# Earlier weight checks on VectorE in group 0, and three steps of GpSimd at other places of the expert stage, in a two-layer gated transformer kernel

## The chip, the cores and the metric

The kernel runs on one core of a Trainium2 chip. The metric is the device time of one execution in microseconds (us), as the median of three. TensorE is called PE below, VectorE DVE, ScalarE ACT, GpSimd POOL, and the queue of SyncE, which issues most of the DMAs, SP.

## The reference

There are T = 2048 tokens of D = 256. Layer 0 is an attention over 64 context keys and a mixture of 16 experts with two chosen for each token; layer 1 is a linear map with a context row and a dense FFN with a hidden width of 1024, whose weights are ternary (-1, 0, 1).

```python
x = x + tanh(g_xattn[0]) * L0_xattn(layernorm(x), ctx, ctx, Wq, bq, Wk, bk, Wv, bv)
x = x + tanh(g_ffn[0])   * L0_ffn(layernorm(x), gate_w, w1, w3, w2)      # 16 experts, top 2
x = x + tanh(g_xattn[1]) * L1_xattn(layernorm(x), ctx, W, b)
x = x + tanh(g_ffn[1])   * L1_ffn(layernorm(x), w1_w, w1_s, ..., w3_w, w3_s)

def L1_ffn(x, ...):                       # tlin(x, w, s) = (x @ w.T) * s
    h = silu(tlin(x, w1_w, w1_s)) * tlin(x, w2_w, w2_s)      # 256 -> 1024
    h = gelu(tlin(h, h1_w, h1_s))                            # 1024 -> 1024
    h = gelu(tlin(h, h2_w, h2_s))                            # 1024 -> 1024
    return tlin(h, w3_w, w3_s)                               # 1024 -> 256
```

## The kernel before

Everything runs in one program, written out by hand for each engine; the order on an engine is the order in which its code is written, and engines wait for each other on semaphores. Three stages follow each other.

**Attention and routing** (to about 76 us) work on four groups of 512 tokens.

**The expert stage** (about 76 to 173 us) is a loop over 47 blocks of 128 rows (`NBLK`) on every engine. POOL gathers the rows of block i (line 641, indirect DMA, into six buffers) once PE has transposed block i-6; PE transposes them, applies the expert's three matrices, and ACT writes the result out, which SP stores. Other work is hung into this loop at fixed block numbers: the tables of lines 62 to 66 say at which i an engine does it. On POOL these are `root_half` (line 566, a power that makes 1/sqrt of a variance; `ROOT2_AT` for the third layer norm, `ROOT3_AT` for the fourth) and `add_row_half` (line 627, adds the context row `crow` to two tiles of X; `ROW_AT`). Each has two halves, q = 0 and 1, and each waits for its own input: `root_half(3, 0)` for the variance that DVE makes in `statistics3_half(0)` at i = 35, `root_half(2, 1)` for the one of i = 37, `add_row_half(1)` for PE's transposes of i = 37. Their results are wanted by `x3_half(1)` (DVE, i = 41) and `normalise4_half(0)` (DVE, i = 43).

**The FFN stage** (from 173 us to the end) works on four groups g of 512 tokens, each with a gated first layer (layer 0 here), `layer` 1, `layer` 2 and the last map to 256 columns. The activations are kept as a high and a low part in fp32r, so each weight tile is used by two matmuls. In layers 1 and 2 PE fills a PSUM bank m by 16 matmuls (lines 1987 and 1988), ACT applies the gelu (line 1533) into one of three buffers `sg`, and DVE makes the high part (`CAST`, line 1259) and the low part (`TENSOR_TENSOR`, line 1261), after which it counts `f_hl[m]` up. The first bank of the next layer needs all eight of these, one by one (line 1986). ACT may run three banks ahead of DVE.

Hung into DVE's loop in group g are steps for the next group: `x2(g + 1)` after m = 1 of layer 1 (lines 1188 to 1194: adds the gathered expert rows to X, one `n_x2` for each of four tiles, and statistics), `low3` after m = 7, `x3` and `normalise4` in layer 2. PE's transposes `T3(g + 1)` stand after m = 6 of layer 1 and wait for those four `n_x2` (line 1902). POOL then makes `root(2, g + 1)` and `add_row(g + 1)` (lines 690 and 691, 128x1024 elements).

The weights come as 44 panels of 128x512 fp32 (256 KB each). SP loads them raw in order (`load_raw`, line 356: at most four on the way); panels 22 to 43 only once PE has finished layer 0 of group 0 (line 482). ACT and DVE round them to fp32r in place. Since rounding loses nothing only where the weights are simple numbers, the kernel checks that: SP loads each panel a second time into one of two buffers `stage` (`load_check`, line 485, all behind the last raw panel in SP's queue; load w waits until check w-2 is done), and DVE compares it with the rounded panel (`check_panel`, line 1229) and writes the count of differences. There are 11 checks a group (`NCHK`), 44 in all; the last ones raise a flag that would start a slower general path. In group 0 the 11 checks stand behind banks m = 5, 6, 7 of layer 1 and all eight of layer 2; in groups 1 to 3 behind all eight of layer 1 and m = 0, 1, 2 of layer 2.

Of the kernel before, what the change touches and what calls it, by code (L numbers as in the profile page):

```python
# [43 lines left out]
FK = F // P  # L44
# [15 lines left out]
JW = DK * P + H  # L60

Y_AT = (28, 29, 31, 32, 34, 35, 37, 38)
ROOT2_AT, ROW_AT, ROOT3_AT = (37, 45), (38, 45), (44, 46)
ADD_AT, STAT_AT = (25, 28, 31, 36), (26, 29, 33, 37)
TURN3_AT, HIGH3_AT, LOW3_AT, PART_AT, X3_AT = (30, 37), (31, 38), (32, 39), (33, 40), (34, 41)
NORM_AT, TURN4_AT, HIGH4_AT, LOW4_AT = (43, 45), (44, 47), (45, 48), (46, 48)
# [4 lines left out]
NCHK = 11  # L71
# [38 lines left out]
def flamingo_kernel(nc, x, ctxT, cols, rows, wq, wkT, wvT, gate, experts, w1T, w2T, panels, consts, identity, out):  # L110
    with ExitStack() as ctx:
# [629 lines left out]
        def _(eng):  # L741
# [446 lines left out]
            def x2(g):  # L1188
                for j in range(TG):
                    row_added(g, j)  # L1190
                    row_statistics(g, j)
                own.done()
                eng.wait_ge(ln_rstd[2], counted(g - 1))
                eng.tensor_scalar(veps[:, 2, :], mv[:, 2, :, 1], EPS, None, ALU.add).then_inc(ln_var[2], 1)

            def low3(g):
                for k in range(DK):
                    eng.wait_ge(n_h3, DK * g + k + 1)
                    ins = eng.tensor_tensor(xTl[:, k, :], bank[6 + k][:, :], xTh[:, k, :].bitcast(F32), ALU.subtract)
                    if k < DK - 1:  # L1200
                        own(ins)
                ins.then_inc(n_l3, 1)

            def x3(g):
                def make(j):
                    if j == 0:
                        eng.wait_ge(n_row, counted(g))
                        eng.wait_ge(ln_rstd[2], counted(g))
                    if j % 2 == 0:
                        eng.wait_ge(n_p1, 2 * g + j // 2 + 1)  # L1210
                    own(eng.scalar_tensor_tensor(tiles(g)(j), bank[6 + j // 2][:, (j % 2) * D:(j % 2 + 1) * D],
                                                 rstd[:, 2, j:j + 1], tiles(g)(j), ALU.mult, ALU.add))

                statistics(eng, own, tiles(g), 3, g, make)

            def normalise4(g):
                eng.wait_ge(ln_rstd[3], counted(g))
                eng.wait_ge(n_T4, counted(g - 1))
                for j in range(TG):
                    eng.tensor_scalar(xn[:, j, :], tiles(g)(j), mv[:, 3, j, 0:1], rstd[:, 3, j:j + 1],  # L1220
                                      ALU.subtract, ALU.mult).then_inc(n_xn, 1)
# [7 lines left out]
            def check_panel(w):  # L1229
                if w >= DVE_PAN:  # L1230
                    eng.wait_ge(act_pan, w + 1 - DVE_PAN)
                eng.wait_ge(dma_chk[w % 2], 16 * (w // 2 + 1))
                to, _ = panel(w)
                eng.scalar_tensor_tensor(stage[:, w % 2, :], stage[:, w % 2, :], 1.0, to.bitcast(F32), ALU.mult,
                                         ALU.not_equal, accum_out=diff[:, w:w + 1]).then_inc(dve_chk, 1)

            def ffn(g, more, general):
# [14 lines left out]
                for layer, h in ((1, hB), (2, hA)):  # L1252
                    for m in range(FK):
                        if layer == 1 and m == 0:

                            eng.wait_ge(f_dma, 16 * g + 16 if g < NG else OUT_DONE + 32 * (g - NG))
                        r = (8 * layer + m) % 3
                        eng.wait_ge(f_act[m], g3 + (layer + 2))
                        own(eng.tensor_copy(h[0][:, m, :], sg[:, r, :]))  # L1259
                        own.done()  # L1260
                        eng.tensor_tensor(h[1][:, m, :], sg[:, r, :], h[0][:, m, :].bitcast(F32),
                                          ALU.subtract).then_inc(f_hl[m], 1)
                        if more and layer == 1 and m == 1:
                            x2(g + 1)
                        if more and layer == 1 and m == 7:
                            low3(g + 1)
                        if more and layer == 2 and m == 2:
                            x3(g + 1)
                        if more and layer == 2 and m == 3:
                            normalise4(g + 1)  # L1270

                        c = 8 * (layer - 1) + m - (FK + FK - NCHK if g == 0 else 0)
                        if not general and 0 <= c < NCHK:
                            check_panel(NCHK * g + c)
                            if NCHK * g + c == NPAN - 1:
                                eng.wait_ge(dve_chk, NPAN)
                                own(eng.reduce_max(flagf[:, 0:1], diff[:, :], AX.X))
                                own.done()
                                eng.tensor_scalar(flagf[:, 0:1], flagf[:, 0:1], 1.0, None, ALU.min).then_inc(dve_flag, 1)
# [28 lines left out]
            for g in range(NG):  # L1308
                ffn(g, g < NG - 1, False)
            eng.wait_ge(pool_flag, 1)  # L1310
            general = eng.value_load(flag[0:1, 0:1], min_val=0, max_val=1)
# [804 lines left out]
```

## Time and profile before

| | |
|---|---|
| median of 3 runs | 519.88 us (518.80 to 521.58) |
| profiled execution | 519.88 us, span 517.8 us |
| PE busy | 485.9 us (94% of the span) |
| DVE busy | 312.4 us (60%) |
| ACT busy | 214.4 us (41%) |
| POOL busy | 149.5 us (29%) |
| TensorE clock granted, mean | 0.974 of full speed |

The span is the time from the first to the last instruction of the profiled execution; 2.1 us of its device time lie around it. Busy time of PE is modelled for pipelined matmuls, so neighbouring matmuls overlap in it. The chain that ended last says which engine a microsecond of delay would have to be on to count; the timelines say what each engine did when, and what it waited for before that. All times in timelines and windows count from the start of the span.

### The profile page before, as it was taken

Reading aid. Unit: us, or ns where it says so; the run is one execution under the profiler, and the core shown is the slowest. Engines: PE = TensorE matmul, PEld = TensorE weight load, DVE = VectorE, ACT = ScalarE, POOL = GpSimd, SP = SyncE. Lnnn points to the kernel's source line nnn. Section 1 sums busy time; section 2 is a strip of 40 time slices with the busy share of each in tenths; the row PEclk is TensorE's granted clock in tenths of the full one; section 3 lists DMA queues with packets and bytes.
Section 4 is the critical chain, followed back from the end, with each engine's and each line's share of the span. In section 5 each row is a group of like instructions: output and inputs, shape, how many; then the busy total and the mean of one; then the engine's idle time right before and its main releaser. Section 6 shows DMA issues by size and latency. Waiting matters only on the chain.

```text
span 517.8 us, 7829 instructions
## 1 busy us (share of the span) xinstructions
PE 485.9 (94%) x2750; PEld 417.0 (81%) x2750; DVE 312.4 (60%) x836; ACT 214.4 (41%) x444; POOL 149.5 (29%) x159
## 2 busy tenths in 40 slices
PE   8898978996899889999999999999999999999996
PEld 8697768885789668888987888897888888788886
DVE  3568876673588566557455964626677634645433
ACT  4379914663467676532245121226322123611210
POOL 1867856656762320201062110116011101000000
PEclk9799977998899999999999999999999999999999
DMA  8945833786672548521141121005032002022101
GB/s 296 330 169 161 282 100 100 198 289 181 198 213 84 184 135 281 163 82 41 42 128 57 52 71 42 0 2 162 22 99 64 0 1 81 3 72 70 42 1 47
DMA packets 34465, 58.82 MB, mean 114 GB/s; under 512 B 4529, under 2 KB 18353, under 8 KB 34354
## 3 DMA queue, kind: packets, MB, share of 16 engines
q1 hardware_dynamic: 29760, 47.12, 27.8%
q0 software_dynamic: 3840, 10.49, 7.4%
q10 hardware_dynamic: 818, 0.61, 0.4%
q8 instruction: 25, 0.41, 0.3%
q14 instruction: 22, 0.18, 0.1%
HBM read 47.85 MB, written 14.42 MB: 120 GB/s over the span
## 4 chain that ended last, share of the span: by engine, by line
PE 84%; DVE 7%; issue 2%; ACT 2%; another core or an unknown queue 1%; DMA 1%; POOL 1%; SPq 0%; DVEq 0%; POOLq 0%
PE bank L1987 23%; PE bank L1988 22%; PE bank L1959 5%; PE bank L1956 5%; PE bank L1559 4%; PE bank L1561 4%; PE bank L1560 4%; PE bank L2020 3%; PE bank L2019 3%; PE bank L1805 2%; PE bank L1645 2%; PE bank L1808 1%; DMA gw<-gate 1%; PE bank L1619 1%
## 5 line engine op out<-in xcount | busy, mean ns | idle before, releaser
L1533 ACT ACTIVATE sg<-bank,colv 128x512 f32<-128x512 f32 x64 | 44.1, 690 | 177.2 <-PE bank L1988 177.2
L1987 PE MATMUL bank<-Ah,Wr 128*128 128x512 f32 x256 | 100.3, 392 | 0.4 <-DVE sg L1242 0.4
L1987 PE MATMUL bank<-Bh,Wr 128*128 128x512 f32 x256 | 99.9, 390 | 0.0
L1988 PE MATMUL bank<-Al,Wr 128*128 128x512 f32 x256 | 99.7, 390 | 0.0
L1988 PE MATMUL bank<-Bl,Wr 128*128 128x512 f32 x256 | 99.7, 389 | 0.0
L1559 PE MATMUL bank<-EL,turned 128*128 (+1 forms) x141 | 47.4, 336 | 12.1 <-ACT yb L1465 9.3
L1987 PEld LDWEIGHTS bank<-Ah,Wr 128*128 128x128 f32 x256 | 48.1, 188 | 11.7 <-DVE sg L1242 1.3
L1988 PEld LDWEIGHTS bank<-Bl,Wr 128*128 128x128 f32 x256 | 48.1, 188 | 9.8
L1988 PEld LDWEIGHTS bank<-Al,Wr 128*128 128x128 f32 x256 | 48.1, 188 | 9.8
L1987 PEld LDWEIGHTS bank<-Bh,Wr 128*128 128x128 f32 x256 | 48.1, 188 | 9.8
L1259 DVE CAST Ah<-sg 128x512 fp32r<-128x512 f32 x32 | 13.6, 426 | 60.0 <-ACT sg L1533 60.0
L564 POOL TENSOR_TENSOR rstd<-veps,mhalf 128x4 f32<-128x4 f32 x6 | 8.4, 1401 | 116.7 <-DVE veps L738 61.1
L1560 PE MATMUL bank<-EH,turned 128*128 (+1 forms) x141 | 41.7, 295 | 0.0
L1077 DVE TENSOR_TENSOR turned<-bank,turned 128x384 fp32r<-128x384 f32 (+2 forms) x51 | 26.6, 523 | 25.0 <-ACT turned L1451 13.9
L1561 PE MATMUL bank<-EH,turned 128*128 (+1 forms) x141 | 41.6, 295 | 0.0
L1559 PEld LDWEIGHTS bank<-EL,turned 128*128 128x128 f32 x141 | 28.6, 203 | 15.2 <-issue 14.7
L1242 DVE SCALAR_TENSOR_TENSOR sg<-bank,colv,sg 128x512 f32<-128x512 f32 x32 | 24.0, 751 | 25.7 <-ACT sg L1519 20.5
L1519 ACT ACTIVATE sg<-bank,colv 128x512 f32<-128x512 f32 x32 | 22.1, 689 | 41.0 <-PE bank L1959 36.9
L1956 PE MATMUL bank<-xTh,Wr 128*128 128x512 f32 x96 | 37.7, 393 | 0.0
L1959 PE MATMUL bank<-xTl,Wr 128*128 128x512 f32 x96 | 37.6, 392 | 0.0
L1259 DVE CAST Bh<-sg 128x512 fp32r<-128x512 f32 x32 | 13.6, 426 | 39.8 <-ACT sg L1533 39.8
L641 POOL DMA_INDIRECT xg<-xb_dram,perm x32 | 30.9, 965 | 17.0 <-PE bank L1808 7.6
(280 smaller groups left out, 1031.2 us busy)
## 6 DMA issues: line engine op xcount, KB each, us to landing
Wraw<-panels SPq DMA_DIRECT2D x44, 256.0 KB
stage<-panels SPq DMA_DIRECT2D x44, 256.0 KB
ES<-experts SPq DMA_DIRECT2D x16, 384.0 KB, 4.9
ys_dram<-yb SPq DMA_DIRECT2D x47, 128.0 KB
ys_dram<-x SPq DMA_DIRECT2D x1, 1920.0 KB, 8.4
X<-x SPq DMA_DIRECT2D x3, 512.0 KB, 7.8
xb_dram<-xb SPq DMA_DIRECT2D x3, 512.0 KB, 5.3
out<-outb SPq DMA_DIRECT2D x3, 512.0 KB
```

The source lines that it names most:

```text
L641: eng.indirect_dma_start(out=rows, out_offset=None, in_=xb_dram, in_offset=bass.IndirectOffsetOnAxis(ap=perm[:, i:i + 1], axis=0)).then_in ...
L1077: eng.tensor_tensor(t_low[b][:, w], bank_t[b][:, w], t_high[b][:, w].bitcast(F32), ALU.subtract).then_inc(b_xl, 1)
L1242: eng.scalar_tensor_tensor(sg[:, m % 3, :], bank[2 * (m % 2) + 1][:, :], colv[:, C_S2 + m:C_S2 + m + 1], sg[:, m % 3, :], ALU.mult, ALU.mu ...
L1259: own(eng.tensor_copy(h[0][:, m, :], sg[:, r, :]))
L1533: eng.activation(sg[:, (8 * layer + m) % 3, :], bank[m % 4][:, :], ACT.Gelu, scale=colv[:, c + m:c + m + 1]).then_inc(f_act[m], 1)
L1559: mm(dst, lhs[0], rhs[1], start=first, stop=False)
L1560: mm(dst, lhs[1], rhs[0], start=False, stop=False)
L1561: return mm(dst, lhs[0], rhs[0], start=False, stop=last)
L1956: mm(dst, w[:, u, k, :], x_high[:, k, :], start=k == 0, stop=False)
L1959: ins = mm(dst, w[:, u, k, :], x_low[:, k, :], start=False, stop=k == DK - 1 and not general)
L1987: mm(bank[m % 4][:, :], Wr[:, base:base + P], h[0][:, k, :], start=k == 0, stop=False)
L1988: ins = mm(bank[m % 4][:, :], Wr[:, base:base + P], h[1][:, k, :], start=False, stop=k == FK - 1 and not general)
```

## The change

Two things are changed. In the expert stage three of POOL's steps stand at other blocks: `root_half(2, 1)` and `add_row_half(1)` come at i = 44 in place of 45, and `root_half(3, 0)` at i = 42 in place of 44. In the FFN stage the 11 checks of group 0 stand where those of the other groups stand: behind m = 0 to 7 of layer 1 and m = 0, 1, 2 of layer 2. The number of checks, their order, the loads on SP and all other engines' code are as before.

```diff
-ROOT2_AT, ROW_AT, ROOT3_AT = (37, 45), (38, 45), (44, 46)
+ROOT2_AT, ROW_AT, ROOT3_AT = (37, 44), (38, 44), (42, 46)
...
-                        c = 8 * (layer - 1) + m - (FK + FK - NCHK if g == 0 else 0)
-                        if not general and 0 <= c < NCHK:
+                        c = 8 * (layer - 1) + m
+                        if not general and c < NCHK:
                             check_panel(NCHK * g + c)
```

What now stands in a row on DVE, in group 0, layer 1, between bank 0 and bank 1 (Bh and Bl are the high and low part of the output of layer 1; `stage` is the buffer of the second load):

```order
 L1259 CAST Bh_53<-sg_58 128x512
 L1261 TENSOR_TENSOR Bl_54<-sg_58,Bh_53 128x512
+L1234 SCALAR_TENSOR_TENSOR stage_61,diff_88<-stage_61,Wr_49 128x512
 L1259 CAST Bh_53<-sg_58 128x512
 L1261 TENSOR_TENSOR Bl_54<-sg_58,Bh_53 128x512
```

The first check comes in between them; behind bank 1 follows `x2(1)`.

DVE before, in the same layer, from the end of `x2(1)` (its last tile's sums and statistics, then the variance `veps`) to bank 2:

```order
L1093 SCALAR_TENSOR_TENSOR X_55<-xn_59,wtop_83,X_55 128x256
L1096 SCALAR_TENSOR_TENSOR X_55<-y2_60,wtop_83,X_55 128x256
L1101 BN_STATS stats_70<-X_55 128x6
L1103 BN_AGGR mv_71<-stats_70 128x2
L1194 TENSOR_SCALAR veps_72<-mv_71 128x4
L1259 CAST Bh_53<-sg_58 128x512
L1261 TENSOR_TENSOR Bl_54<-sg_58,Bh_53 128x512
```

And now:

```order
L1093 SCALAR_TENSOR_TENSOR X_55<-xn_59,wtop_83,X_55 128x256
L1096 SCALAR_TENSOR_TENSOR X_55<-y2_60,wtop_83,X_55 128x256
L1101 BN_STATS stats_70<-X_55 128x6
L1103 BN_AGGR mv_71<-stats_70 128x2
L1194 TENSOR_SCALAR veps_72<-mv_71 128x4
L1234 SCALAR_TENSOR_TENSOR stage_61,diff_88<-stage_61,Wr_49 128x512
L1259 CAST Bh_53<-sg_58 128x512
L1261 TENSOR_TENSOR Bl_54<-sg_58,Bh_53 128x512
L1234 SCALAR_TENSOR_TENSOR stage_61,diff_88<-stage_61,Wr_49 128x512
```

The check of bank 1 stands behind `x2(1)`, and each of banks 2, 3 and 4 has one behind its pair, where there was none. Five checks have left the banks of layer 2 from m = 3 on.

POOL in the expert stage, from the gather of block 39 to the end of the loop (xg and xg_more are the buffers of the gathers, two adjacent gathers stand in one row with x2):

```order
 L641 DMA xg_173<-xb_dram,perm_85 128x256 x2
 L641 DMA xg_more_174<-xb_dram,perm_85 128x256 x2
+L569 TENSOR_TENSOR rstd_73<-veps_72,mhalf_74 128x2
 L641 DMA xg_173<-xb_dram,perm_85 128x256 x2
 L569 TENSOR_TENSOR rstd_73<-veps_72,mhalf_74 128x2
-L641 DMA xg_173<-xb_dram,perm_85 128x256
-L569 TENSOR_TENSOR rstd_73<-veps_72,mhalf_74 128x2
 L630 TENSOR_TENSOR X_55<-X_55,crow_69 128x512
-L641 DMA xg_173<-xb_dram,perm_85 128x256
+L641 DMA xg_173<-xb_dram,perm_85 128x256 x2
 L569 TENSOR_TENSOR rstd_73<-veps_72,mhalf_74 128x2
```

`root_half(3, 0)` now stands ahead of the gathers of blocks 43 and 44, and `root_half(2, 1)` and the context row's addition ahead of those of blocks 45 and 46.

## Rows read from the trace of the kernel before

**Rows 1.** The page: the chain that ended last by engine (section 4), one group (section 5).

```profile
PE 84%; DVE 7%; issue 2%; ACT 2%; another core or an unknown queue 1%; DMA 1%; POOL 1%; SPq 0%; DVEq 0%; POOLq 0%
...
L564 POOL TENSOR_TENSOR rstd<-veps,mhalf 128x4 f32<-128x4 f32 x6 | 8.4, 1401 | 116.7 <-DVE veps L738 61.1
```

**Rows 2.** Timeline of SP: start us, us, engine, line, operation, out<-in, count.

```profile
174.79 34.38 SPq L360 DMA_DIRECT2D Wraw<-panels  x28
...
209.22 0.91 SPq L488 DMA_DIRECT2D stage<-panels  x2
```

**Rows 3.** Busy time by window: DMA share and GB/s are the last two columns.

```profile
209.00:213.00 4.00, 4.00 (x19) 3.32 (x18) 1.12 (x2) 2.62 (x5) 0.00 (x0) 1.00 0.90 292
213.00:213.50 0.50, 0.50 (x4) 0.40 (x3) 0.24 (x1) 0.50 (x2) 0.00 (x0) 1.00 0.49 188
```

**Rows 4.** Timeline of DVE, layer 1 of group 0; in brackets idle time before, and releaser.

```profile
199.22 0.69 DVE L1261 TENSOR_TENSOR Bl<-sg,Bh 128x512 fp32r<-128x512 f32 x1
199.83 0.48 DVE L1093 SCALAR_TENSOR_TENSOR X<-xn,wtop,X 128x256 f32<-128x256 f32 x1
...
205.05 0.48 DVE L1096 SCALAR_TENSOR_TENSOR X<-y,wtop,X 128x256 f32<-128x256 f32 x1
...
206.33 0.42 DVE L1259 CAST Bh<-sg 128x512 fp32r<-128x512 f32 x1
...
214.33 0.69 DVE L1234 SCALAR_TENSOR_TENSOR stage<-stage,Wr 128x512 f32<-128x512 f32 x1
```

**Rows 5.** Timeline of DVE, layer 2 of group 0.

```profile
228.70 0.43 DVE L1259 CAST Ah<-sg 128x512 fp32r<-128x512 f32 x1 [1.86 <-ACT sg L1533]
...
242.76 0.68 DVE L1234 SCALAR_TENSOR_TENSOR stage<-stage,Wr 128x512 f32<-128x512 f32 x1
...
244.43 0.69 DVE L1234 SCALAR_TENSOR_TENSOR stage<-stage,Wr 128x512 f32<-128x512 f32 x1
```

**Rows 6.** Timeline of PE, end of layer 1 and first bank of layer 2, group 0.

```profile
215.97 1.04 PE L1904 MATMUL bank<-ident,X 128*128 128x128 f32 x8
...
223.69 0.39 PE L1987 MATMUL bank<-Bh,Wr 128*128 128x512 f32 x1
```

**Rows 7.** Timelines of DVE and POOL where POOL adds a context row.

```profile
155.10 1.55 DVE L1056 TENSOR_SCALAR X<-X,alpha,beta 128x256 f32<-128x256 f32 x1
...
158.50 0.40 DVE L1056 TENSOR_SCALAR X<-X,alpha,beta 128x256 f32<-128x256 f32 x1
...
217.09 2.49 POOL L676 TENSOR_TENSOR X<-X,crow 128x1024 f32<-128x1024 f32 x1 [9.24 <-PE bank L1904]
217.36 2.77 DVE L1261 TENSOR_TENSOR Bl<-sg,Bh 128x512 fp32r<-128x512 f32 x1
220.05 0.68 DVE L1234 SCALAR_TENSOR_TENSOR stage<-stage,Wr 128x512 f32<-128x512 f32 x1
```

**Rows 8.** Timeline of SP, and narrow windows (GB/s last), around two transfers that ran alone.

```profile
174.00:174.25 0.25, 0.25 (x3) 0.21 (x2) 0.00 (x0) 0.00 (x0) 0.00 (x0) 1.00 0.62 201
...
174.79 0.33 SPq L360 DMA_DIRECT2D Wraw<-panels  x1
...
215.06 0.33 SPq L488 DMA_DIRECT2D stage<-panels  x1
...
217.00:217.25 0.25, 0.25 (x3) 0.21 (x2) 0.25 (x1) 0.25 (x1) 0.16 (x1) 1.00 0.21 74
```

**Rows 9.** Busy time by window in the block stage: PEclk is third from the end.

```profile
119.60:124.00 4.40, 0.80 (x7) 0.59 (x6) 0.56 (x1) 0.61 (x2) 2.25 (x3) 1.00 0.53 161
125.80:129.00 3.20, 3.20 (x17) 3.20 (x17) 1.73 (x4) 1.46 (x4) 1.77 (x3) 0.50 0.84 232
74.50:84.40 9.90, 8.11 (x48) 7.53 (x46) 3.36 (x14) 2.47 (x7) 5.68 (x6) 0.50 0.27 79
```

**Rows 10.** Timelines of DVE and PE in the block stage.

```profile
151.27 0.17 DVE L1108 TENSOR_SCALAR veps<-mv 128x2 f32<-128x2 f32 x1
...
162.29 0.38 PE L1805 MATMUL bank<-ident,xg 128*128 128x128 f32 x2
```

## The prediction

> **What bounds the kernel now.** I read the page's chain first: it lies on PE for 84% of the span [rows 1], so an edit on another engine counts only where it makes PE wait. Then I asked, for each moved step, which transfer or engine it waits for and who waits behind it. In the FFN stage that led from DVE to SP's queue. SP issues the last 28 raw panels from 174.79 to 209.17 without a pause worth naming, and only then, at 209.22, the first two loads of the checks [rows 2]. The first check ran at 214.33, right behind DVE's own work for bank 5 of layer 1 [rows 4], and waited for nothing. The change asks for its data one bank ahead of the pair that was over at 199.83 [rows 4], so before 197. SP's code is the same, and its loads hang on PE and on the panels, so they do not come earlier. DVE will stand still for them, with the low parts of layer 1 behind it.
>
> **When the first check can run (T0).** At 209.22 raw panels and two check loads are on the way together: 292 GB/s from 209 to 213 and 188 GB/s in the next half microsecond, where it runs out [rows 3]. The last 256 KB are those of the second check load: 94 KB of them in that half microsecond, the other 162 KB at 292 GB/s take 0.55 us, so the first load's last byte comes at 212.45. From last byte to a released wait I take the store that ran alone: it moved its last bytes before 174.25 and SP went on at 174.79, 0.5 us later [rows 8]. T0 = 213.0. Bounds: 212.5 (no such delay) and 214.3 (the check did run then).
>
> **DVE from T0 on**, all of it work that waits ready, since ACT may be three banks ahead:
> - Check 0, 0.61 us, and the pair of bank 1, 1.07 us. A check and a pair together are 244.43 - 242.76 = 1.67 us [rows 5]; a pair without its check is what is left, and the check's own share is that of its start to the next start, as for the TENSOR_TENSOR 199.22 to 199.83 [rows 4]. `x2(1)` starts at 214.7.
> - `x2(1)`: 206.33 - 199.83 = 6.5 us [rows 4], to 221.2. Its fourth `n_x2` comes 205.05 + 0.48 - 199.83 = 5.7 us after its start, at 220.4. PE's T3 started at 215.97 before [rows 6] and waits for that: PE is about 4 us late at bank 7.
> - Six times check and pair (checks 1 to 6, banks 2 to 7), 10.0 us, to 231.2.
> - POOL's `root(2, 1)`, 1.4 us [rows 1], starts when `x2(1)` is over, and its context row, 2.49 us [rows 7], follows it (T3 is over by then). This now falls into DVE's hurry, from 222.7 to 225.2, where check 2 is due at 222.9. In the trace a TENSOR_TENSOR that should take 0.69 us took 2.77 beside that same addition, and the next started 0.47 us after the addition's end [rows 7]. So DVE goes on at 225.7 in place of 223.5: +2.2 us. Bounds: 0, and 2.2. I take the upper one since a TENSOR_SCALAR with one tensor was held as well (1.55 us for 0.40, beside the half-size addition of the expert stage [rows 7]), so all of DVE's operations here look exposed.
> - The low part of bank 7 is there at 231.2 + 2.2 = 233.4, and 0.2 us more for its end and the handover: 233.6.
>
> The Trainium skill (SBUF — State Buffer, section "SBUF: two separate sides") says that VectorE and GpSimd share one pair of SBUF ports as an exclusive lock, which a VectorE operation with two SBUF inputs or in a two-port mode needs and which whoever starts first keeps for the whole instruction. By that rule the check itself, with two SBUF inputs, is held and the addition costs the full 2.2 us; had only the pair's TENSOR_TENSOR been held, as the row alone shows, it would be the one of bank 3, due at 223.9, and the cost 1.1 us. The rows are with the rule.
>
> **Does the load of each check keep up?** SP issued load 2 at 215.06, 0.73 us after check 0 started [rows 4, 8]; its last bytes moved before 217.25 [rows 8], and with 0.5 us for the wait it is ready about 3.3 us after the check two places before. Two steps of DVE are 3.34 us. It just fits; if a load takes 0.3 us more, three pairs of steps cost +0.9. I take 0 and keep 0.9.
>
> **What PE sees.** Layer 2's first bank needs the low parts one by one. Its last two matmuls started at 223.69 [rows 6] and now start at 233.6: **+9.9 us**. The 4 us at T3 are part of that, not beside it. All later matmuls follow back to back, and nothing later on PE has slack to give back. In layer 2 DVE waited 1.86 us for a gelu although it had a check there [rows 5], so it gets level in one or two banks, and the five checks that leave layer 2 free time that nobody waits for: 0.
>
> **PE's clock.** PE stands or works thinly from 216 to 220 and again from 226 to 233. Before, after the thin stretch 119.6 to 124.0 (0.80 us busy in 4.4), the granted clock was 0.50, that is 1.2 GHz, from 125.8 to 129.0 [rows 9]. A first slow stretch of that length would lie in the time in which PE is paced by DVE, and costs nothing; a second one, begun by the pacing, reaches into dense matmuls, where each microsecond of it costs half. Bounds 0 and half of 3.2, 1.6; I take the middle, **+0.8**.
>
> **The steps on POOL in the expert stage.** `root_half(3, 0)` now waits for a variance that DVE writes at 151.27 [rows 10], ahead of the gather of block 43; the gathers of 45 and 46 come behind `root_half(2, 1)` and the addition. By the rows I estimate the gather of 45 some 4 us later than before, at about 157.2; a lone 256 KB load needed 2.2 us to its last byte [rows 8], 0.5 for the wait, and the gather moves half as much, so it is there by 161, ahead of PE's transposes at 162.29 [rows 10]. No wait is added. DVE's steps stand where they stood, and the earlier half of the root is wanted only at block 43. If the addition, which moves by about half a microsecond, no longer holds DVE at 155.10 [rows 7], up to 0.3 us is gained; a gather that does come late costs about as much as it is late, 1 us at the most. I take 0.
>
> **Sum.** The profiled execution took 519.88 us, which is also the median of the three. 519.88 + 9.9 + 0.8 = **530.6 us**.
>
> **Rivals.**
> - *Short.* The addition on POOL holds nobody, the first load is there at 212.5, the clock does not fall into dense work: 519.88 + 9.9 - 2.2 - 0.5 = 527.1. For it: only one kind of pair was seen held here. Against: both rows of [rows 7].
> - *Long.* PE's clock stays down. Before, it stayed at 0.50 for 9.9 us, from 74.5 to 84.4, with PE 8.1 us busy in it [rows 9]. If such a stretch begins in the pacing and lies over 5 to 8 us of dense work, it costs 2.5 to 4 us in place of 0.8, with the loads' 0.9 at most beside it: 532.3 to 534.7. Against: the more usual stretches are of 3.2 us.
> - *Not slower.* DVE's wait for the first check is covered. The place is `dma_chk[0]` behind bank 0 of layer 1. The last low part of layer 1 comes 20.6 us after T0, and PE wanted it at 223.69, so up to T0 = 203.1 the change costs nothing, and from there on each microsecond of T0 costs one. Then only the expert stage's steps are left: 519.6 to 519.9. Against: the load is not even issued by 209.22 [rows 2], and nothing in the change moves that. It would need the second load of a panel to come out of SP's queue ahead of the raw ones.
>
> **How the numbers follow.** Forecast (528 to 532.3): 0.75. Short (below 528, but slower): 0.09. Long: 0.12. Not slower: 0.04. The range of 527.3 to 533.5 takes in the lower bounds of T0 and of the addition together, and above it 1.3 us of T0, the rest of the clock's 1.6 and a part of the loads' 0.9. A measurement of this kernel can tell about 0.5% from no change, 2.6 us. All cases but the last are above that: slower 0.96, within 0.03, faster 0.01.
>
> **What the changed kernel's profile would show.** DVE idle for some 16 us ahead of the first L1234, which starts near 213.0 and has the DMA as its releaser; PE's T3 late by about 4 us, waiting on DVE's L1096; the PE matmuls of layer 2's first bank spread over some 8 us, with waits on DVE's L1261; POOL's L676 with a DVE operation of over 2 us beside it; PEclk at 0.50 somewhere between 221 and 238; from the second bank of layer 2 on every row of PE later by the same 10 to 11 us. In the expert stage every row of PE as before within 0.3 us. The prediction is wrong if the first L1234 starts before 210, if PE goes on into layer 2 while DVE still makes the low parts, or if PE's delay shrinks again in groups 1 to 3.

## The result, and the profile after

The changed kernel takes 535.49 us (median of 4 runs, 533.00 to 536.22) against 520.34 us of the kernel before on the same chip (4 runs, 518.80 to 521.58): ratio 1.028 (1.024 to 1.033), so 12 to 17 us slower. The sign and the mechanism of the prediction hold, its size doesn't: 530.6 us was forecast, with a range up to 533.5. The profiled execution took 533.13 us, its span is 531.0 us. Medians here and below are taken over all runs of a kernel, ratios without those runs that lie more than 1.5% above its fastest.

The page of the changed kernel: the chain that ended last, by engine, and the group of the checks.

```profile
PE 76%; DVE 9%; DMA 6%; issue 3%; ACT 3%; another core or an unknown queue 1%; POOL 1%; SPq 1%; DVEq 0%; POOLq 0%
...
L1234 DVE SCALAR_TENSOR_TENSOR stage<-stage,Wr 128x512 f32<-128x512 f32 x44 | 32.4, 735 | 17.9 <-DMA stage<-panels 17.8
```

PE's share of the chain fell from 84% [rows 1] to 76%, those of DVE and DMA grew, and all 44 checks together waited 17.9 us for loads, 17.8 of them in one place. The timelines of SP and DVE show that place (in layer 1 of group 0; the columns are those of [rows 4]).

```profile
174.05 35.16 SPq L360 DMA_DIRECT2D Wraw<-panels  x28
...
195.23 0.69 DVE L1261 TENSOR_TENSOR Bl<-sg,Bh 128x512 fp32r<-128x512 f32 x1
213.69 0.69 DVE L1234 SCALAR_TENSOR_TENSOR stage<-stage,Wr 128x512 f32<-128x512 f32 x1 [17.77 <-DMA stage<-panels]
...
215.38 0.48 DVE L1093 SCALAR_TENSOR_TENSOR X<-xn,wtop,X 128x256 f32<-128x256 f32 x1
...
221.87 0.69 DVE L1234 SCALAR_TENSOR_TENSOR stage<-stage,Wr 128x512 f32<-128x512 f32 x1
...
223.55 2.88 DVE L1234 SCALAR_TENSOR_TENSOR stage<-stage,Wr 128x512 f32<-128x512 f32 x1
...
226.36 0.41 DVE L1259 CAST Bh<-sg 128x512 fp32r<-128x512 f32 x1
...
233.51 0.69 DVE L1261 TENSOR_TENSOR Bl<-sg,Bh 128x512 fp32r<-128x512 f32 x1
```

SP is through with the raw panels at 209.21, where it was at 209.17 before [rows 2], and issues the first load of a check at 209.26. DVE had been ready at 195.9 and stands still for 17.77 us. Then it works off `x2(1)` and the pairs and checks one behind the other up to 234.2. The check at 223.55 takes 2.88 us where its neighbours take 0.69. The reason stands in POOL's timeline:

```profile
222.05 1.41 POOL L564 TENSOR_TENSOR rstd<-veps,mhalf 128x4 f32<-128x4 f32 x1 [37.31 <-DVE veps L1194]
223.45 2.42 POOL L676 TENSOR_TENSOR X<-X,crow 128x1024 f32<-128x1024 f32 x1
```

PE's timeline in the same stretch: the transposes T3 (L1903), then the end of layer 2's first bank.

```profile
216.52 0.41 PE L1903 MATMUL bank<-ident,X 128*128 128x128 f32 x2 [1.12 <-DVE X L1096]
...
221.14 0.69 PE L1903 MATMUL bank<-ident,X 128*128 128x128 f32 x2 [0.88 <-DVE X L1096]
...
230.90 0.50 PE L1986 MATMUL bank<-Bh,Wr 128*128 128x512 f32 x1 [0.94 <-DVE Bl L1261]
...
232.58 0.54 PE L1986 MATMUL bank<-Bh,Wr 128*128 128x512 f32 x1 [0.94 <-DVE Bl L1261]
...
234.26 0.80 PE L1986 MATMUL bank<-Bh,Wr 128*128 128x512 f32 x1 [0.71 <-DVE Bl L1261]
234.85 0.63 PE L1987 MATMUL bank<-Bl,Wr 128*128 128x512 f32 x1
...
239.12 0.63 PE L1987 MATMUL bank<-Bl,Wr 128*128 128x512 f32 x1
```

The eight transposes that stood in one row before [rows 6] now come by twos with a wait each, and the first bank of layer 2 takes its low parts one by one as DVE delivers them. Its last pair begins at 234.26, where it began at 223.69 [rows 6]. From there PE waits for nobody, yet its matmuls stand 0.43 us apart and not 0.23. The table by windows shows why (columns: window, its length, busy time of PE, PEld, DVE, ACT, POOL, then PEclk, DMA share and GB/s).

```profile
215.00:219.60 4.60, 1.28 (x7) 0.43 (x5) 4.32 (x12) 2.24 (x4) 0.00 (x0) 0.96 0.20 57
219.60:225.90 6.30, 5.42 (x15) 4.05 (x16) 6.09 (x12) 2.17 (x4) 3.82 (x2) 0.50 0.11 42
225.90:233.00 7.10, 5.21 (x21) 3.42 (x19) 6.96 (x17) 4.90 (x10) 0.00 (x0) 0.98 0.41 120
233.00:239.40 6.40, 5.69 (x14) 4.12 (x13) 4.71 (x12) 0.69 (x1) 0.00 (x0) 0.50 0.43 122
239.40:245.00 5.60, 5.60 (x36) 5.07 (x36) 1.73 (x4) 0.69 (x1) 0.00 (x0) 0.97 0.11 40
```

TensorE's granted clock is 0.50 (1.2 GHz) twice, for about 6.3 us each time, once behind 4.6 us in which PE was busy for 1.28, and once behind the stretch in which DVE paced it. From 239.4 on the matmuls are at full speed and stay there.

### Where the 14 us went

Executions differ by some microseconds in what stands ahead of that point, so I count from one point on: the start of the last matmul of layer 0 in group 0 (190.17 before, 189.44 after). All numbers are microseconds behind it; "last pair" is the last two matmuls of layer 2's first bank, "next" the first matmul of the next step on PE (L1558), "group 1" the first matmul of layer 0 in group 1, "rest" what is left of the span from there.

| kernel | check 0 | last pair | next | group 1 | rest |
|---|---|---|---|---|---|
| before | 24.16 (no wait) | 33.52 | 37.60 | 70.83 | 256.80 |
| changed | 24.25 | 44.82 | 51.58 | 84.83 | 256.73 |
| changed_again | 23.87 | 44.49 | 51.22 | 84.47 | 256.07 |
| steps_only2 | 24.21 (no wait) | 33.54 | 37.62 | 70.88 | 255.93 |
| checks_only2 | 23.76 | 44.32 | 50.52 | 83.75 | 255.84 |
| no_data2 | 6.39 (no wait) | 33.53 | 37.61 | 70.87 | 255.87 |
| filled2 | 23.24 | 43.82 | 48.04 | 81.27 | 255.71 |
| filled_again | 23.71 | 44.40 | 48.63 | 81.87 | 255.90 |
| filled_late_add | 23.17 | 42.52 | 46.74 | 79.97 | 255.81 |
| lone_first | 23.76 | 44.42 | 48.65 | 81.90 | 256.05 |
| first_at_1 | 24.54 | 36.89 | 42.72 | 75.94 | 256.07 |
| first_at_2 | 24.44 | 35.06 | 39.27 | 72.49 | 256.01 |
| first_at_3 | 24.87 | 33.80 | 38.01 | 71.27 | 255.84 |
| two_ahead | 6.78 (no wait) | 35.55 | 39.76 | 72.99 | 256.05 |

The changed kernel reaches group 1 14.0 us later: 11.3 at the last pair, and 2.7 between it and the next step (6.76 for 4.08 us). The rest of the run is the same within 0.1 us. Its FFN stage began 0.73 us earlier than in the trace of before (172.22 for 172.95), so the profiled execution is 519.88 + 14.0 - 0.7 = 533.2 us by this count; measured were 533.13.

### The profile page after: what moved, and what is told of

Same layout as the page of the kernel before. It is cut to its first block, busy times and chain, and to the rows that moved or that the text cites. A ratio compares the mean times of both kernels' runs of the same rounds, so it can differ in the third digit from the quotient of the medians.

```text
span 531.0 us, 7829 instructions
## 1 busy us (share of the span) xinstructions
PE 490.7 (92%) x2750; PEld 418.2 (79%) x2750; DVE 311.9 (59%) x836; ACT 214.6 (40%) x444; POOL 150.3 (28%) x159
## 4 chain that ended last, share of the span: by engine, by line
PE 76%; DVE 9%; DMA 6%; issue 3%; ACT 3%; another core or an unknown queue 1%; POOL 1%; SPq 1%; DVEq 0%; POOLq 0%
PE bank L1986 19%; PE bank L1987 19%; PE bank L1958 5%; PE bank L1558 4%; PE bank L1955 4%; PE bank L1560 4%; PE bank L1559 4%; DMA Wraw<-panels 3%; PE bank L2019 3%; PE bank L2018 3%; PE bank L1804 2%; PE bank L1644 2%; DMA X<-x 1%; DVE stage L1234 1%
## 5 line engine op out<-in xcount | busy, mean ns | idle before, releaser
L1986 PE MATMUL bank<-Bh,Wr 128*128 128x512 f32 x256 | 102.0, 398 | 2.6 <-DVE Bl L1261 2.6
L1986 PE MATMUL bank<-Ah,Wr 128*128 128x512 f32 x256 | 101.7, 397 | 0.4 <-DVE sg L1242 0.4
L1987 PE MATMUL bank<-Bl,Wr 128*128 128x512 f32 x256 | 101.4, 396 | 0.0
L1987 PE MATMUL bank<-Al,Wr 128*128 128x512 f32 x256 | 100.9, 394 | 0.0
L1558 PE MATMUL bank<-EL,turned 128*128 (+1 forms) x141 | 47.4, 336 | 13.3 <-ACT yb L1464 7.8
L1234 DVE SCALAR_TENSOR_TENSOR stage<-stage,Wr 128x512 f32<-128x512 f32 x44 | 32.4, 735 | 17.9 <-DMA stage<-panels 17.8
L1558 PEld LDWEIGHTS bank<-EL,turned 128*128 128x128 f32 x141 | 28.6, 203 | 16.7 <-issue 16.4
```

Of the source, the lines that this page charges most:

```text
L1558: mm(dst, lhs[0], rhs[1], start=first, stop=False)
L1986: mm(bank[m % 4][:, :], Wr[:, base:base + P], h[0][:, k, :], start=k == 0, stop=False)
L1987: ins = mm(bank[m % 4][:, :], Wr[:, base:base + P], h[1][:, k, :], start=False, stop=k == FK - 1 and not general)
```

## The experiments

**The theory.** Behind bank 0, check 0 waits for a load that SP issues only behind the last raw panel; then DVE's work (20.6 us from check 0) paces PE up to the last pair, POOL's addition holds it for 2.2 us in that chain, and PE's clock falls and costs what is left. **The rivals:** the steps in the expert stage have a part in it; DVE's added work between the banks costs it even without the wait; the missing time is loads that don't keep up, or the first load shares the DMA engines with the second; and it is something other than the clock that makes the matmuls behind the last pair slow. steps_only2, checks_only2, no_data2 and filled2 ran on one chip; filled_late_add, first_at_1, first_at_3 and two_ahead on another; changed_again, filled_again, lone_first and first_at_2 on a third; each beside the kernel before (505.28, 517.06 and 505.68 us there).

### steps_only2: the steps of the expert stage alone

```diff
-ROOT2_AT, ROW_AT, ROOT3_AT = (37, 45), (38, 45), (44, 46)
+ROOT2_AT, ROW_AT, ROOT3_AT = (37, 44), (38, 44), (42, 46)
```

(to the kernel before)

> GpSimd's three steps of the expert stage at their new places, the checks of group 0 at their old ones. Theory A (the whole loss comes from DVE's wait for the data of the first check, and from PE's clock behind it): 520.3 us, within 0.5% of the kernel before, PE's rows of the expert stage within 0.3 us of before. Theory B (the part of the loss that the prediction missed, some 4 us, is the late gathers of the expert stage): 524 us, with PE or ACT waiting for a gather behind block 43.

Measured: 505.13 us, ratio 0.999 (0.996 to 1.002), and every point of the table up to group 1 as before within 0.05 us (the rest is 0.9 us shorter, as in the other kernels on other chips). The POOL steps are worth nothing that can be measured.

### checks_only2: the place of the checks alone

```diff
-ROOT2_AT, ROW_AT, ROOT3_AT = (37, 44), (38, 44), (42, 46)
+ROOT2_AT, ROW_AT, ROOT3_AT = (37, 45), (38, 45), (44, 46)
```

(to the changed kernel)

> The checks of group 0 at their new places, GpSimd's steps at their old ones. Theory A: 535.5 us, the same as the changed kernel. Theory B: 530 to 531 us, 4 to 5 us faster than the changed kernel.

Measured: 517.55 us, ratio 1.027 (1.021 to 1.034), and group 1 later by 12.9 us. The whole loss comes from the checks. From check 0 to the last pair it is 20.56 us, and 20.57 in the changed kernel.

### no_data2: the checks at the new places, without loads to wait for

The 11 checks of group 0 compare the rounded panel with itself, and their loads are left out, so 11 panels are not compared with what was loaded; DVE's instructions stay where the change puts them.

```diff
-                eng.wait_ge(dma_chk[w % 2], 16 * (w // 2 + 1))
+                if w >= NCHK:
+                    eng.wait_ge(dma_chk[w % 2], 16 * ((w - NCHK) // 2 + 1))
                 to, _ = panel(w)
+                other = stage[:, w % 2, :] if w >= NCHK else to.bitcast(F32)
...
-                for w in range(NCHK * g, NCHK * (g + 1)):
+                for w in range(NCHK * max(g, 1), NCHK * (g + 1)):
```

(`other` takes the place of `stage` as the second tensor of the comparison)

> The changed kernel, in which the 11 checks of group 0 compare the rounded panel with itself and wait for no load, and SP does not load these 11 panels a second time: the comparison of 11 panels is left out, DVE's instructions, their sizes and their order are as in the changed kernel. Theory A (the wait for the data is the cost): 520.3 us, within 1%, no DVE wait in layer 1 of group 0 but for the gelu. Theory C (it is the five more checks in layer 1, and the context row's addition that holds DVE, whether the data is there or not): 523 to 531 us, with PE waiting on DVE's low parts at the first bank of layer 2.

Measured: 505.13 us, ratio 0.999 (0.996 to 1.003). In DVE's timeline check 0 stands right behind the pair of bank 0, without a wait:

```profile
182.25 0.69 DVE L1236 SCALAR_TENSOR_TENSOR stage<-Wr 128x512 f32<-128x512 f32 x1
```

The last pair comes at +33.53, as before. The same 11 instructions at the same places cost nothing when their data is there. So the loss is the wait and what follows from it, and not the work that was put between the banks.

### filled2 and filled_again: the changed kernel with PE kept busy in its waits

```diff
+            def fill(n, h):
+                for _ in range(n):
+                    mm(bank[5][:, :], Wr[:, FK * PANEL:FK * PANEL + P], h, start=True, stop=True)
...
                 for j in range(TG):
+                    if g == 1:
+                        fill(5, hA[0][:, 0, :])
...
                                 if m == 0:
+                                    if g == 0 and layer == 2 and k >= 4:
+                                        fill(4, h[0][:, 0, :])
                                     eng.wait_ge(f_hl[k], g3 + layer + 1)
```

The added matmuls write a bank that nobody reads before it is written anew: five ahead of each of the four waits of T3(1), four ahead of each of the last four low parts of layer 1. They stand in time in which PE waited.

> The changed kernel with 5 idle matmuls of 512 columns ahead of each of the four waits of T3 in group 0, and 4 ahead of the waits for the low parts k = 4 to 7 in layer 2's first bank, into a bank that nobody reads: 36 in all, each shorter than the wait it stands in. They only keep PE busy. Theory A (PE's clock at 1.2 GHz in dense matmuls behind the waits costs 2.7 us in the profiled execution, and more in others): 531 to 532.5 us, PEclk at 1.00 from 215 to 245. Theory D (the clock costs nothing, since the slow stretches lie in PE's waits): 535.5 us or more.

Measured: 517.03 us, ratio 1.025 (1.018 to 1.032). The ratio can't be told from that of checks_only2, but the trace can. One window over all of DVE's chain (columns as above):

```profile
200.00:228.00 28.00, 27.32 (x130) 21.28 (x129) 25.01 (x57) 10.72 (x19) 3.84 (x2) 1.00 0.34 90
```

And PE's timeline at the last pair (L1900 is the filling, L1993 and L1994 are the pairs):

```profile
219.93 1.09 PE L1900 MATMUL bank<-Bh,Wr 128*128 128x512 f32 x4
221.04 0.50 PE L1993 MATMUL bank<-Bh,Wr 128*128 128x512 f32 x1
221.37 0.40 PE L1994 MATMUL bank<-Bl,Wr 128*128 128x512 f32 x1
221.61 0.40 PE L1993 MATMUL bank<-Bh,Wr 128*128 128x512 f32 x1
```

The clock stays at 1.00, and from the last pair to the next step it is 4.22 us, where the changed kernel needs 6.76 and the kernel before 4.08. The chain up to the last pair, 20.58 us from check 0, is not touched. So it was the clock, at 6.76 - 4.22 = 2.5 us; on the chip of this run, where checks_only2 needs 6.20, it is 2.0 us.

The pair was run once more on the third chip, as filled_again beside the changed kernel itself, changed_again:

> The changed kernel once more, for a second profile and a tighter ratio. Theory A (9.9 us of chain after the data, the data some 1 us later than forecast, and PE's clock): from the end of the first layer of group 0 to the first bank of group 1 about 84 us for the 70.8 of before, 13 to 14 us more; ratio 1.025 to 1.028. Theory F (there is a further loss outside the FFN stage that the first profile did not show): ratio over 1.029, with a later start of the FFN stage than in the kernel before.

> The kernel with the 36 filling matmuls once more, beside the changed kernel on the same chip. Theory A: the clock stays at 1.00, the stretch to the first bank of group 1 is 81 to 82 us, 2.5 to 3.5 us less than in the changed kernel, and the time 0.5 to 0.7% lower (ratio to before 1.020 to 1.022). Theory D (filling gives nothing back in the time): the same ratio as the changed kernel within 0.2%.

Measured: changed_again 518.55 us, ratio 1.026 (1.021 to 1.031); filled_again 516.00 us, 1.022 (1.017 to 1.026). The ratios are 0.0044 apart, which is 2.2 us, the points of group 1 2.6 us (84.47 and 81.87). The intervals still overlap, so by the times alone this is likely and not shown; the traces carry it. The slow stretches of changed_again, by windows, lie where those of the changed kernel lie, and are as long:

```profile
202.60:209.00 6.40, 5.32 (x14) 4.05 (x15) 6.16 (x13) 2.04 (x4) 3.72 (x2) 0.50 0.12 41
...
216.50:223.00 6.50, 5.83 (x14) 4.29 (x14) 4.50 (x10) 0.69 (x1) 0.00 (x0) 0.50 0.40 110
```

### filled_late_add: the addition taken out of DVE's hurry

```diff
                 eng.wait_ge(n_T, counted(g))
+                if g == 1:
+                    eng.wait_ge(f_hl[7], 3)
```

(in POOL's `add_row`, to filled2: the addition waits for the last low part of layer 1)

> The kernel with the 36 filling matmuls, and with GpSimd's addition of the context row in group 0 put behind DVE's last low part of layer 1, where DVE no longer hurries. Theory A (the addition holds DVE's check for 2.2 us on the path): from the end of the first layer to the first bank of group 1 2.2 us less than in the filled kernel, ratio to before 0.4% lower than there, 1.021 for 1.025, and no L1234 longer than 0.7 us in layer 1 of group 0. Theory E (the addition's overlap hides elsewhere, for instance in the wait for the next gelu): no difference from the filled kernel.

Measured: 524.75 us, ratio 1.013 (1.006 to 1.021). From check 0 to the last pair it is 19.35 us for 20.58 of filled2: 1.2 us less, and not 2.2. Two rows of DVE's timeline:

```profile
225.54 0.69 DVE L1236 SCALAR_TENSOR_TENSOR stage<-stage,Wr 128x512 f32<-128x512 f32 x1 [0.83 <-DMA stage<-panels]
...
233.50 1.98 DVE L1236 SCALAR_TENSOR_TENSOR stage<-stage,Wr 128x512 f32<-128x512 f32 x1
```

The hold is gone from the chain; the addition now starts at 232.53 and holds the check at 233.50, behind the last low part, where nobody waits. But check 3 waited 0.83 us for its load, which SP had issued at 221.99: 3.55 us from issue to the check's start. With the hold at check 2 that lateness had been hidden, since the load of check 3 was issued behind check 1 and had the held 2.2 us on top. So the two terms are not independent: the hold of 2.2 us covers a load that is 0.8 us late, and taking it away gives back 1.2 us. The trace of this run has 1.3 us less than filled2 up to group 1 (79.97 and 81.27) and a rest that is the same. By the trace it is 9.1 us slower than before, a ratio of 1.018, which the measured interval holds; the ratio itself, 1.013, lies lower than that, and the runs don't show why.

### first_at_1, first_at_2, first_at_3: the first check behind bank 1, 2, 3

```diff
-                        c = 8 * (layer - 1) + m
-                        if not general and c < NCHK:
+                        c = 8 * (layer - 1) + m - (1 if g == 0 else 0)
+                        if not general and 0 <= c < NCHK:
```

(to the changed kernel, here for first_at_1; 2 and 3 in place of the 1 in the others)

> The changed kernel with the first check of group 0 one bank later: behind bank 1 and behind x2(1), the other ten behind the banks that follow. Theory A (cost = what of DVE's chain behind the first check's data is later than PE wants it): x2(1) and T3 are in time; six pairs and five checks (10.1 us) and the held addition (2.2) come after the data, the last low part 36 us after the end of the first layer's matmuls in place of 33.5: 2.8 us, with PE's clock 3 to 4.5 us slower than before (ratio 1.006 to 1.009). Theory C (each check moved into layer 1 costs for itself): four of five moved checks are left, so four fifths of the changed kernel's loss, 10 us or more (ratio over 1.02).

> The changed kernel with the first check of group 0 behind bank 2 of layer 1. Theory A: data at about 24.2 us after the first layer, then five pairs and four checks (7.8 us), the held addition (2.2) and 0.2: the last low part is wanted at 33.5 and comes at 35.0, so 1.5 us slower (2 at most), between the 0.4 us of the first check behind bank 3 and the 5.1 of behind bank 1; ratio 1.003. Theory C (each moved check costs): 60% of the loss, 8 us, ratio 1.016.

> The changed kernel with the first check of group 0 behind bank 3 of layer 1. Theory A: DVE still waits for the data, some 4 us, but has only four pairs and three checks behind it (6.7 us, 2.2 for the held addition), done before PE wants the last low part: no change from before (ratio within 0.3% of 1), with a DVE wait for the load in the trace. Theory C: two fifths of the loss, 5 us (ratio 1.01).

Measured: first_at_1 523.96 us, ratio 1.012 (1.005 to 1.019), group 1 later by 5.1 us, which is more than the 3 to 4.5 expected (3.4 at the last pair, where 2.8 were expected, and 1.75 of clock); first_at_2 505.33 us, 0.998 (0.995 to 1.001), by 1.7 us; first_at_3 517.27 us, 1.000 (0.997 to 1.004), by 0.4 us. The check waits in all of them; in first_at_3:

```profile
213.06 0.69 DVE L1234 SCALAR_TENSOR_TENSOR stage<-stage,Wr 128x512 f32<-128x512 f32 x1 [6.26 <-DMA stage<-panels]
```

A wait of 6.26 us (4 were expected) that costs 0.4 us: what counts is not how long DVE stands but how much stands behind the check. Once `x2(1)` and bank 1 are ahead of it, the chain from check 0 to the last pair is a number of pairs of 1.67 us, the hold of 2.1 us and 0.2 us for the end: 6 x 1.67 + 2.3 = 12.3 us (measured 36.89 - 24.54 = 12.35), 5 x 1.67 + 2.3 = 10.65 (10.62), 4 x 1.67 + 2.3 = 9.0 (8.93). In first_at_1 the clock fell as well, as this window shows (within it, it was 0.50 from 227.8 to 231.0), and the next step came 5.83 us behind the last pair:

```profile
227.00:232.00 5.00, 5.00 (x15) 3.99 (x16) 3.37 (x8) 0.69 (x1) 0.00 (x0) 0.66 0.48 127
```

In first_at_2 and first_at_3 it did not (4.21). For first_at_2 trace and times don't agree well: 1.7 us in the trace, while the interval of the times allows at most 0.7 us. The table compares with a trace of the kernel before from another chip, which is one way in which this can come about, though steps_only2 and no_data2, on a third chip, have the points of that trace within 0.05 us; it isn't settled.

### two_ahead: two of the loads ahead of the raw panels

```diff
                 if n == FIRST_PAN:

                     eng.wait_ge(f_pe[FK - 1], 1)
+                    eng.wait_ge(n_x2, TG)
+                    load_check(0)
+                    load_check(1)
                 load_raw(eng, n)
```

(to the changed kernel; checks 0 and 1 leave their old place in SP's queue)

> The changed kernel, in which SP issues the loads of checks 0 and 1 ahead of raw panel 22 in place of behind panel 43; all other loads, and DVE's order, as in the changed kernel. Theory A: checks 0 and 1 find their data, x2(1) and T3 are in time, and DVE now waits for load 2 behind bank 2, some 24.5 us after the first layer: the last low part is some 2 us late, with the clock 2 to 3.5 us slower than before (ratio 1.004 to 1.007). Theory C: as the changed kernel, ratio 1.025 or more.

Measured: 520.96 us, ratio 1.005 (1.001 to 1.009), group 1 later by 2.2 us. SP's and DVE's timelines:

```profile
190.19 0.80 SPq L481 DMA_DIRECT2D stage<-panels  x2
191.04 19.95 SPq L360 DMA_DIRECT2D Wraw<-panels  x22
211.08 10.11 SPq L481 DMA_DIRECT2D stage<-panels  x5
...
196.54 0.68 DVE L1237 SCALAR_TENSOR_TENSOR stage<-stage,Wr 128x512 f32<-128x512 f32 x1
...
214.70 0.69 DVE L1237 SCALAR_TENSOR_TENSOR stage<-stage,Wr 128x512 f32<-128x512 f32 x1 [6.55 <-DMA stage<-panels]
```

Checks 0 and 1 wait for nothing, and `x2(1)` with them; check 2 now waits for a load behind the raw panels, with banks 3 to 7 behind it. This is the rival *Not slower* made true: of 14.0 us 11.8 are gone, by nothing but the place of two loads in SP's queue. The other 2.2 are the same mechanism two checks later.

### lone_first: the first load without the second beside it

```diff
-                if w >= 2:
-                    eng.wait_ge(dve_chk, w - 1)
+                if w >= 1:
+                    eng.wait_ge(dve_chk, max(1, w - 1))
```

(to filled2: load 1 is issued only behind check 0)

> The kernel with the filling matmuls, in which SP issues the load of check 1 only once check 0 is done, so that the first load does not share the DMA engines with the second. Theory G (the forecast had the first load land ahead of the second; they share the engines and end nearly together, which is why it took 4.2 to 4.7 us from issue to check): 3.7 us from issue to the first check, 0.5 to 1 us less, and the stretch to group 1 shorter by as much (80.5 us). Theory H (the raw panels ahead of it set the time): 4.2 to 4.7 us as before.

Measured: 514.63 us, ratio 1.017 (1.011 to 1.022); the points of the table are those of filled_again within 0.1 us. The timelines of SP and DVE:

```profile
195.14 0.43 SPq L488 DMA_DIRECT2D stage<-panels  x1
...
199.51 0.69 DVE L1234 SCALAR_TENSOR_TENSOR stage<-stage,Wr 128x512 f32<-128x512 f32 x1 [17.28 <-DMA stage<-panels]
```

And the windows behind the issue:

```profile
195.10:198.60 3.50, 3.50 (x17) 2.88 (x16) 0.00 (x0) 0.00 (x0) 0.00 (x0) 1.00 0.79 267
198.60:199.10 0.50, 0.50 (x4) 0.42 (x3) 0.00 (x0) 0.00 (x0) 0.00 (x0) 1.00 0.13 49
```

Still 4.37 us from issue to check, where filled_again, with both loads, has 200.14 - 195.83 = 4.31. So holding the second load back gains nothing here, as Theory H has it. It is one trace for each, though, and the same stretch differs by more than the 0.5 us in question from trace to trace: in changed_again, with both loads, it took 3.39 us (193.54 to 196.93). What sets it is argued and not tested: from 195.1 to 199.1, 3.5 x 267 + 0.5 x 49 = 959 KB were moved, the 256 KB of the load and some 700 KB that must be raw panels issued ahead of it, of which up to four may be on the way.

## Why the prediction was wrong, and where it was right

- **What bounds, and the first check's place in SP's queue:** right. DVE stood 17.77 us (some 16 forecast), with the DMA as releaser; with no data to wait for (no_data2) the loss is gone, with two loads issued early (two_ahead) all but 2.2 us of it. One reading under it is wrong: SP does not issue the 28 raw panels "without a pause worth naming". In the trace of before six go out, then SP stands still for 12 us, of which 9.5 are put down to PE's layer 0, and then come the other 22 (two windows of SP's timeline, and its waits):

```profile
174.79 3.57 SPq L360 DMA_DIRECT2D Wraw<-panels  x6
...
190.59 18.59 SPq L360 DMA_DIRECT2D Wraw<-panels  x22
...
SPq L360 <- PE bank L1959: 9.5, 1, 9.5
```

  The forecast's times hold all the same, since T0 was taken from the issue at 209.22. But it is PE's layer 0 and the 22 panels behind it that put the first load there, and there are 12 us ahead of them in which SP issued nothing.
- **T0 = 213.0:** too early by 1.4 us when counted from the end of layer 0 (24.25 for 22.83). 0.8 of it is SP: it issued load 0 at +19.82 and not at +19.05, as the raw panels took 35.16 us for 34.38 [rows 2]. The other 0.6 is the load: 4.43 us from issue to check, 3.8 forecast. That split isn't a fixed one: in changed_again, the same kernel, the load went out at +20.48 and took 3.39 us. The forecast worked its 3.8 us out from the bytes, as if the first load were through when all but 256 KB had moved. The tail in the changed kernel, by windows, is longer than the one of [rows 3]:

```profile
211.50:213.00 1.50, 1.50 (x9) 1.23 (x8) 0.00 (x0) 0.00 (x0) 0.00 (x0) 1.00 0.92 333
213.00:213.50 0.50, 0.50 (x4) 0.42 (x3) 0.00 (x0) 0.00 (x0) 0.00 (x0) 1.00 0.46 172
213.50:213.75 0.25, 0.25 (x3) 0.21 (x2) 0.06 (x1) 0.00 (x0) 0.00 (x0) 1.00 0.23 90
213.75:214.00 0.25, 0.25 (x3) 0.21 (x2) 0.25 (x1) 0.00 (x0) 0.00 (x0) 1.00 0.15 57
```

  The check starts while bytes still move, by then those of the second load, so both loads seem to end close together. The other runs with the checks behind the raw panels have check 0 at +23.2 to +24.9; the upper bound, 214.3, is +24.13. Not one of them is as early as 22.83.
- **DVE's chain, 20.6 us:** right, 20.57 us, and 20.56 to 20.69 in the five other runs with the same chain (checks_only2, changed_again, filled2, filled_again, lone_first). Its parts fit too: check 0 and the pair of bank 1 1.69 us (1.68 forecast), `x2(1)` 6.5 us, a check and a pair 1.67 us.
- **POOL's addition, +2.2 us:** right in place and size. The check at 223.55 went on at 226.36, 2.2 us later than its 0.6 us would have had it. But the term isn't worth its length: taken away, it gave 1.2 us and not 2.2 (filled_late_add), since a load was late behind it.
  By the rule of the Trainium skill that the prediction quotes (SBUF — State Buffer, section "SBUF: two separate sides") a check, with two SBUF inputs, is held by a POOL operation that started first. The trace agrees: 2.88 us for 0.69, started 0.10 us behind the addition.
- **The loads keep up, 0 us:** right for the changed kernel, and for a reason that the forecast didn't have. It allowed 2.7 us from the issue of a load to a released wait (215.06 to 217.25, and 0.5); filled_late_add shows 3.55 us, and a wait of 0.83 us for it. In the changed kernel the hold covered that.
  The Trainium skill (DMA: Bandwidth & Descriptors, section "Anatomy of one DMA — SWDGE (gpsimd) path") fits a DMA that GpSimd issues as about 2.0 us and its bytes at 436 GB/s; that gives an estimate of 2.6 us for 256 KB. The 3.55 us here, of a load that SP issued, with the check's own start in it, are longer.
- **PE at T3 is about 4 us late, as part of the chain:** right, with T0's 1.4 us on top: bank 7 began at 221.48 (+32.04), and at 216.77 (+26.60) before, 5.4 us later.
- **PE's clock, +0.8 us:** this is the step that failed. It measured 2.7 us. The forecast took the length of a slow stretch from one row, 3.2 us at 0.50 [rows 9], called it the more usual one and laid half of it over dense work. The stretch was 6.4 us (233.0 to 239.4), and 5.1 us of it lay behind the last pair, at half speed: 2.6 us, nearly all of the 2.7. Its place, and that the first stretch costs nothing, were right. The trace of before had five slow stretches: three of about 3.3 us, the 9.9 us of [rows 9], and one of 6.4 us over dense matmuls, which the forecast doesn't name:

```profile
20.20:26.60 6.40, 6.40 (x25) 4.96 (x25) 2.39 (x10) 1.23 (x3) 6.23 (x8) 0.50 0.72 276
```

  With those two the upper bound of 1.6 us was too low. The rival *Long* has this mechanism, 2.5 to 4 us of clock and 532.3 to 534.7 us, at a chance of 0.12; the trace fits it, while the median lies above even its end. With T0's 1.4 us beside the clock the range ended too low.
- **The steps on POOL in the expert stage, 0 us:** right (steps_only2). In the changed kernel the gather of block 45 came at 155.92, and PE waited for none of the moved steps:

```profile
150.55 0.72 POOL L569 TENSOR_TENSOR rstd<-veps,mhalf 128x2 f32<-128x2 f32 x1 [3.81 <-DVE veps L1108]
...
154.47 1.27 POOL L630 TENSOR_TENSOR X<-X,crow 128x512 f32<-128x512 f32 x1
155.92 1.02 POOL L641 DMA_INDIRECT xg<-xb_dram,perm  x1 [0.17 <-PE bank L1807]
```

  The new wait of `root_half(3, 0)` is there, 3.81 us long, and it was covered.
- **Nothing is given back:** right. The rest of the run is 256.73 us for 256.80.

In numbers, by the trace: 9.9 + 1.4 (T0) + 2.7 (clock) = 14.0 us where 10.7 were forecast, which gives 533.9 us from the 519.88 of the trace of before. The median, 535.49, is 1.6 us more than that, and 2.4 us more than the profiled execution, whose 533.13 us lie inside the forecast's range. What those 2.4 us are is open, as no trace shows them; the runs of this kernel lie between 533.0 and 536.2, their mean clocks between 0.952 and 0.966, and the ratio's interval holds the 14.0 us.

## What to carry to other kernels

A step that waits for a transfer is as early as its transfer in the issuing queue: before moving the step, look at what stands ahead of the load (here a wait for PE's layer 0, and behind it 22 panels, 18.6 us). What a wait costs is then counted from its end, as the work that stands behind it on its engine less the slack of whoever wants that work: 17.8 us of standing still cost 11.3 here, and 6.3 us cost 0.4 three banks later. And where a stall leaves TensorE working in pieces, add the clock: a slow stretch may lie over the dense work behind the stall, and it is sized by the longest such stretch that the trace shows as well as by the shortest.

## What the runs showed that I had not expected

- **The clock's slow stretches behind a stop-and-go differ in length.** Twice 6.3 us in the changed kernel, about 6.4 us each in its run on another chip, 3.2 and 6.4 us in checks_only2; the second of the two cost 2.1 to 2.7 us in the changed kernel, changed_again and checks_only2 (6.76, 6.73 and 6.20 us for 4.08); in first_at_1, with a shorter paced stretch, the only one was of 3.2 us and the loss 1.8 us (5.83 for 4.08). Matmuls that compute nothing, put into the waits, kept the clock at 1.00 and gave 2.6 us.
- **A load behind others took 3.4 to 4.8 us** from issue to use (4.43 in the changed kernel, 3.39 in changed_again, 4.75 in first_at_1), and a later one, with little beside it, 3.55 us, all for 256 KB.
- **The kernel before took 520.3, 505.3, 517.1 and 505.7 us in the four sets of runs.** The traces of the kernels in these sets place most of the difference ahead of the FFN stage: that began at 172.95 in the first set, between 157.7 and 162.5 in the second and fourth, and at 171.2 to 175.2 in the third, and its layer 0 in group 0 took 14.7 to 18.9 us, while from group 1 on all took 255.7 to 256.8 us. What causes it is not known from these runs. Ratios are to be taken within a set.
- **None of the kernels beat the one before.** By their times steps_only2, no_data2, first_at_2 and first_at_3 can't be told from it.
